# Source sums of a graph kernel with the message terms as weights, added up in transposed layout

## The reference

```python
h_edge = jnp.concatenate([x[src], x[dst]], axis=-1)
m_ij = jax.nn.relu(h_edge @ W_interact + b_interact)
m_i = jax.ops.segment_sum(m_ij, src, num_segments=x.shape[0])
m_i = m_i / jnp.asarray(math.sqrt(AVG_DEGREE), dtype=x.dtype)
out = x + jax.nn.relu((x + m_i) @ W_update + b_update)
```

## Time and profile before

| what | value |
|---|---|
| three timed runs | 1555.04, 1557.01, 1558.96 us; median 1557.01 |
| profiled execution, span from first to last instruction | 1552.8 us |
| PE, DVE, ACT, POOL busy | 85%, 87%, 61%, 60% of the span |

### The profile page before, as it was taken

How to read it: one execution, slowest core, us unless ns; L and a number is a source line. 1 busy time by engine, 2 the same in 40 slices (tenths; PEclk the granted TensorE clock), 3 DMA queues, 4 the chain that set the end, 5 groups by cost and what they waited for, 6 DMA issues and landing times.

```text
span 1552.8 us, 39671 instructions
## 1 busy us (share of the span) xinstructions
PE 1322.9 (85%) x14762; PEld 1128.6 (73%) x14762; DVE 1343.5 (87%) x3914; ACT 940.1 (61%) x1835; POOL 931.1 (60%) x942
## 2 busy tenths in 40 slices
PE   1512877999999989899999679889999999999997
PEld 1311655777777767677767578889899999998887
DVE  6968878999999945777866679999999999999998
ACT  2642766778777942010001358878888878887886
POOL 5253803777773005677770147777777777777773
PEclk9965889999999999999999789999999999999999
DMA  4003554475646218799987234444444444444442
GB/s 120 1 1 89 198 232 150 152 253 180 228 177 211 113 50 278 257 310 305 305 280 220 72 77 122 138 121 126 128 127 120 128 127 126 134 131 126 127 120 61
DMA packets 121785, 241.63 MB, mean 156 GB/s; under 512 B 20184, under 2 KB 74601, under 8 KB 121594
## 3 DMA queue, kind: packets, MB, share of 16 engines
q1 hardware_dynamic: 95179, 187.74, 36.1%
q0 software_dynamic: 24832, 50.78, 13.2%
q10 hardware_dynamic: 1584, 0.59, 0.1%
HBM read 169.09 MB, written 73.14 MB: 156 GB/s over the span
## 4 chain that ended last, share of the span: by engine, by line
PE 46%; DVE 35%; issue 7%; SPq 4%; DMA 4%; ACT 3%; POOL 2%; DVEq 1%; ACTq 0%; POOLq 0%
PE ps L1262 13%; PE ps L1468 12%; DVE room L2186 6%; PE ps L1244 5%; DVE hot L1809 4%; PE ps L1233 3%; PE ps L1479 3%; PE ps L1459 3%; DVE slab L2230 2%; SPq L663 2%; PE ps L1302 2%; DVE ps L2222 2%; DVE keys L1935 2%; DVE keys L1934 2%; DVE hot L1804 2%
## 5 line engine op out<-in xcount | busy, mean ns | idle before, releaser
L1014 ACT ACTIVATE slab<-ps 128x980 f16<-128x980 f32 x256 | 321.2, 1277 | 118.7 <-PE ps L1233 102.9
L925 POOL DMA_INDIRECT cells<-b_rows,work x236 | 245.1, 1039 | 74.9 <-issue 67.7
L1468 PE MATMUL ps<-slab,room 125*128 125x128 f16 x3538 | 236.0, 221 | 36.0 <-DVE room L2186 33.5
L1244 PE MATMUL ps<-slab,room 128*128 128x320 f16 x1568 | 252.2, 301 | 0.1
L1468 PEld LDWEIGHTS ps<-slab,room 125*128 125x128 f16 x3538 | 206.5, 98 | 49.5 <-DVE room L2186 49.1
L1123 ACT ACTIVATE lnw<-iota_w,keys 128x126 f32<-128x126 f32 x750 | 242.4, 389 | 0.0
L1459 PE MATMUL ps<-inv,hot 125*128 125x128 f16 x1800 | 224.3, 220 | 5.2 <-DVE hot L2176 5.1
L1262 PE MATMUL ps<-slab,room 128*128 128x320 f16 x1568 | 226.9, 301 | 0.0
L1233 PE MATMUL ps<-hot 128*128 128x245 bf16 x1024 | 160.6, 282 | 50.4 <-DVE hot L1809 39.0
L889 POOL DMA_INDIRECT hot<-t_rows,pairs x160 | 165.8, 1036 | 55.2 <-issue 48.1
L1262 PEld LDWEIGHTS ps<-slab,room 128*128 128x128 f16 x1568 | 153.2, 98 | 59.4 <-issue 2.7
(11 more groups left out here) (371 smaller groups left out, 2442.4 us busy)
## 6 DMA issues: line engine op xcount, KB each, us to landing
slabs_d<-slab SPq DMA_DIRECT2D x14, 3920.0 KB, 13.9
slab<-slabs_d SPq DMA_DIRECT2D x98, 560.0 KB, 5.5
hot<-lane_d SPq DMA_DIRECT2D x50, 576.0 KB
inv<-inv_row SPq DMA_DIRECT2D x32, 160.0 KB, 7.0
keys<-up_d SPq DMA_DIRECT2D x25, 160.0 KB
room<-up_d SPq DMA_DIRECT2D x25, 160.0 KB
cells<-b_rows,work POOLq DMA_INDIRECT x236
t_rows<-room SPq DMA_DIRECT2D x1, 3200.0 KB, 13.7
```

Of the source, the lines that this page charges most:

```text
L925: p.indirect_dma_start(rows_g[gi % RS][:, j, :], None, b_rows, bass.IndirectOffsetOnAxis(ap=node_t[:, t:t + 1], axis=0)).then_inc(e_gath[g ...
L1014: a.activation(slab[par][:, :, u * UB * BW:(u + 1) * UB * BW].rearrange("p h (k d) -> p k h d", k=UB), psum_unit(u).rearrange("p k (h d) - ...
L1244: last = t.matmul(ps[:, 4 + s % 2, 0:SC], table[:, h, term, :], slab[s % 2][:, h, :], start=k == 0, stop=k == HI * HALVES - 1)
L1468: last = t.matmul(to, end_hot[g // 3][0:BN, u:u + P], bt[0:BN, bt_at(tile, w), k, :], start=False, stop=w == w1 - 1 and k == HALVES - 1)
```

## The change

The source sum swaps its operands. Before, the source one-hot was the weights (128 edges by 126 nodes) and both message terms moved side by side (256 columns), which left the two terms in two halves, nodes on the partitions. Now each term is the weights (128 edges by 128 features) in a matmul of its own and the one-hot moves (125 columns); both terms add up in the same 125 columns of PSUM, features on the partitions. So `whole_sum` and `turn_sum` are gone, and `keep_sum` reads the bank directly, where `whole_sum` stood. The wait of `low_term` on `e_psum` is dropped too; the high term, for which it waits, has waited for the same count.

```diff
             def source_sum(gi):
                 b, g = divmod(gi, GB)
                 pe.wait_ge(e_low, gi + 1)
                 pe.wait_ge(e_dvehot if g in DVE_HOTS else e_srchot, hots(gi))
                 if g == 0 and b > 1:
-                    pe.wait_ge(e_whole, b - 1)
+                    pe.wait_ge(e_added, b - 1)
                 for j in range(GT):
-                    last = t.matmul(ps[0:BE, 4 + b % 2, 0:2 * D], src_hot[gi % 6][:, j, :],
-                                    msg[gi % 3][:, j, :, :].rearrange("p k f -> p (k f)"),
-                                    start=g == 0 and j == 0, stop=g == GB - 1 and j == GT - 1)
+                    for k in range(HALVES):
+                        last = t.matmul(ps[:, 4 + b % 2, 0:BN], msg[gi % 3][:, j, k, :], src_hot[gi % 6][:, j, 0:BN],
+                                        start=g == 0 and j == 0 and k == 0,
+                                        stop=g == GB - 1 and j == GT - 1 and k == HALVES - 1)
                 last.then_inc(e_psum, 1)
-
-            def turn_sum(b):
...
-                t.transpose(ps[:, 7, 2 * P:2 * P + BN], block_sum[0:BN, :], ident[0:BN, 0:BN]).then_inc(e_turned, 1)
...
-                if g == 2 and b > 1:
-                    turn_sum(b - 2)
...
             def low_term(gi):
                 dve.wait_ge(e_msg, gi + 1)
-                if gi > 2:
-                    dve.wait_ge(e_psum, gi - 2)
...
-            def whole_sum(b):
+            def keep_sum(b):
                 dve.wait_ge(e_psum, (b + 1) * GB)
-                if b:
-                    dve.wait_ge(e_turned, b)
-                v.tensor_reduce(out=block_sum[0:BN, :], in_=ps[0:BN, 4 + b % 2, 0:2 * D].rearrange("p (k f) -> p f k", k=2),
-                                op=ALU.add, axis=AX.X).then_inc(e_whole, 1)
-
-            def keep_sum(b):
-                dve.wait_ge(e_turned, b + 1)
                 to = hT[:, b * BN:(b + 1) * BN]
-                v.scalar_tensor_tensor(out=to, in0=ps[:, 7, 2 * P:2 * P + BN], scalar=settle[:, 0:1], in1=to,
+                v.scalar_tensor_tensor(out=to, in0=ps[:, 4 + b % 2, 0:BN], scalar=settle[:, 0:1], in1=to,
                                        op0=ALU.mult, op1=ALU.add).then_inc(e_added, 1)
...
-                if g == 2 and b > 1:
-                    keep_sum(b - 2)
                 if g == 4 and b:
-                    whole_sum(b - 1)
+                    keep_sum(b - 1)
...
             low_term(NGR - 1)
-            keep_sum(NB - 2)
-            whole_sum(NB - 1)
             keep_sum(NB - 1)
```

More of the change, by code:

```diff
@@ L395, in gnn_kernel @@
         g_hot = scaled[:, D:D + BN]
-        block_sum = scaled[:, 0:D]
         s_const = sem("s_const")
@@ L496, in gnn_kernel @@
         e_low = sem("e_low")
-        e_whole = sem("e_whole")
-        e_turned = sem("e_turned")
         e_psum = sem("e_psum")
@@ L1476, in source_sum @@
                 if g == 0 and b > 1:
-                    pe.wait_ge(e_whole, b - 1)
+                    pe.wait_ge(e_added, b - 1)
                 for j in range(GT):
-                    last = t.matmul(ps[0:BE, 4 + b % 2, 0:2 * D], src_hot[gi % 6][:, j, :],
-                                    msg[gi % 3][:, j, :, :].rearrange("p k f -> p (k f)"),
-                                    start=g == 0 and j == 0, stop=g == GB - 1 and j == GT - 1)
+                    for k in range(HALVES):
+                        last = t.matmul(ps[:, 4 + b % 2, 0:BN], msg[gi % 3][:, j, k, :], src_hot[gi % 6][:, j, 0:BN],
+                                        start=g == 0 and j == 0 and k == 0,
+                                        stop=g == GB - 1 and j == GT - 1 and k == HALVES - 1)
                 last.then_inc(e_psum, 1)
-            def turn_sum(b):
-                pe.wait_ge(e_whole, b + 1)
-                if b:
[L1487 to L1490, removed]
-                t.transpose(ps[:, 7, 2 * P:2 * P + BN], block_sum[0:BN, :], ident[0:BN, 0:BN]).then_inc(e_turned, 1)
             def update(c):
@@ L1509, in _ @@
                     general_edges()
-                if g == 2 and b > 1:
-                    turn_sum(b - 2)
                 if g == GB - 1 and b - 2 in LAST_BLOCK:
                     update(LAST_BLOCK.index(b - 2))
-            turn_sum(NB - 2)
             source_sum(NGR - 4)
@@ L1518, in _ @@
             source_sum(NGR - 1)
-            turn_sum(NB - 1)
             update(NC - 1)
```

## The result

Six timed runs of each kernel: 1555.38 us before (median, 1551.94 to 1558.96), 1544.77 after (1542.91 to 1549.98). The ratio, with its 95% interval, is 0.9935 [0.9918, 0.9952]: 0.65% or 10.1 us faster, between 7.5 and 12.8. The forecast was 6.2 us.

A forecast was written before the change was run, and what follows sets the result against it. The prediction took a loop of DVE and ACT to bound the third stage's ordinary blocks, with gathers close. 4.9 us (blocks to 48) + 1.3 (end) = 6.2 off the 1552.8 span, plus 4.2, gave 1550.8 us; range 1545.5 to 1555.

The forecast's parts named there:

- The loop: Third stage: DVE runs g2's low term to g5's row add, then ACT to g2's high term; blocks 8-48 gain 4.9 us.
- The wait in g2: Ordinary blocks, DVE's low term of g2 waiting for ACT's high term: 0.11 us becomes 0.37 in the block shown.
- the add in g2: DVE's add into `hT` leaves g2: its 0.26 us is worth nothing in ordinary blocks, counts fully in update blocks.
- The swap in g4: In DVE's half, the add (0.26 us) takes the reduction's place (0.33), shortening every block by 0.07 us.
- PE: Source sum on PE: six narrow matmuls at 56 ns take 0.50 us against 0.49 for three wide ones; no change.
- the slower rival: PE becomes the bound if narrow matmuls cost 98 ns each: 0.5 us more a block, 1577 us in all; 8%.
- The end: After the last row add: last high term starts 0.50 us earlier, final reduction and transposition drop out, 0.84; together 1.3 us.
- The step that failed: Blocks 0 to 7 of the third stage: nothing counted, as DVE's savings go into waiting for block 7's late gather.
- The base: Span of 1552.8 us and median of 1557.0, 4.2 above it; the same 4.2 was added to the changed kernel's span.
- The full gain: Rival: g2's low term does not wait for ACT, DVE gains 0.33 us in every block, POOL-capped at 10; 1545.7 us; 12%.
- The small part failing: Rival: the 0.07s are lost to g4's add cost or late gathers; 3.4 us left, 1553.6 us, no measurable change; 20%.

The follow-up runs named there:

- the two paddings: Changed kernel plus one add-sized DVE instruction on a scratch tile, at the end of g2 (1548.5 us, 0.9949) or in g4 ahead of the add (1558.7 us, 1.0013).
- the repeats: Unchanged kernels run again: before, second and third time, 1554.6 us (0.9983) and 1553.6 us (1.0); after, second time, 1545.7 us (0.995).
- The second timing: The changed kernel, unaltered, timed again against a copy of the kernel before on the same chip: 1545.7 us, 0.995, 7.8 us faster.
- the split early: ACT's split of `a` moved a block earlier, ahead of the high term of g5: on the changed kernel 1536.7 us (0.9892), on the kernel before 1551.1 us (0.9982).

## Why the prediction was right in its mechanism and short in its size

- **The loop** held. The wait in g2 was forecast as 0.37 us in the block shown and is 0.36 in one like it; the 0.26 of the add in g2 is worth nothing in ordinary blocks and all of it in update blocks, as the two paddings show. The swap in g4 is 0.08 a block where 0.07 was forecast. Forecast 4.9 us for blocks 8 to 48, measured 5.4, with 511.1 to 511.3 before and 505.7 to 505.9 after.
- **PE** held: six narrow matmuls step by 56 to 57 ns in the mean and cost what three wide ones did. Nothing in the traces speaks for the slower rival. The 81 ns of the Trainium skill (TensorE: Matmul & The Clock Gate, Back-to-back issue gap) are not what these matmuls took. PE has come near, though: in block 48 it holds up the row add of g3 by 0.32 us, in front of the longer wait for ACT.
- **The end** held: 1.4 us against 1.3, and the same up to the last add in the repeats.
- **The step that failed** is "For blocks 0 to 7 I count nothing: what DVE wins there it waits longer for the late gather in block 7." It took the gathers' arrival as given. In fact it moved: the waits for gathers are 4.5 to 5.7 us in three runs of before and 1.1 and 2.2 in two of after. Every kernel with the add, or a padding of its size, at the end of g2 and the row one-hot whole has 3.9 to 7.6 us of them, every one without has 0.6 to 2.2. In time that is 101.8 to 106.7 us for blocks 0 to 7 with the add there (mean of seven 103.7), 99.4 to 101.9 without (mean of five 100.4, the 2.8 of the update taken out). The first run of after lies high among these, at 101.9, since its row adds stood 3.4 us behind PE in block 3. Between before and after themselves it is some 3.0 us, on three executions and two: the term that the forecast put at nothing. With it the sum is 4.9 + 1.3 + 3.0 = 9.2, where 10.1 and 7.8 were measured. The gathers beside the row one-hots make up this difference: over 0.94 us each they took 3.9, 4.9 and 7.2 us in the runs of before, 2.0 and 1.9 in those of after. The padding in g2 bears this out less well: there they took 2.1, and what it lost in blocks 0 to 7 lies with other gathers.
- **The base** was off as well. The forecast stood on three runs with a median of 1557.0, 4.2 us above the span; six runs gave 1555.4, and a run lies 1.8 us above its own span. That put the predicted time 1.6 us too high, whatever the change did; with the gathers it took the measured 1544.8 to 0.7 us below the range. The second timing, 1545.7, lies just inside.
- **The full gain** gave 1545.7, nearly the measured time, by a mechanism that did not happen: it needs DVE not to wait for ACT, and DVE waits 11.9 us. The small part failing is out, too.

What stays open is how the add at the end of g2 makes the gathers later. That the row one-hot holds a gather that starts behind it is shown. That the add merely shifts when the two meet (it stands 0.26 us of DVE time ahead of the row one-hot) is not enough. Over the whole stage I took the gathers that start 0.27 to 0.31 us behind the start of a whole row one-hot. In the kernels without an add or padding at the end of g2 all 21 of them took 1.31 to 1.36 us. In those with one, 15 of 103 did, 77 took 1.53 to 1.55, and eleven, all in blocks 0 to 7, took 2.38 or 2.39. Block 7 with the split early shows it at the offset of 0.28 us at which the kernel before had 2.39:

```profile
1012.79 0.81 DVE L2163 TENSOR_SCALAR hot<-hot,lane_c 125x2304 f16<-125x2304 f16 x1
1013.07 1.34 POOL L922 DMA_INDIRECT cells<-b_rows,work  x1 [0.30 <-issue]
```

Nor does the period of a block separate the two sets: ordinary blocks take 11.80 to 12.25 us in the kernels with an add or padding there and 11.97 to 12.50 in those without, and the padding in g2 leaves them at the 12.17 of the changed kernel. What makes the difference at the same offset is not shown.

## What to carry to other kernels

When two engines set the pace in turn, ask of each saved instruction in which engine's half it stood: the same 0.26 us cost 2 us at one place and 11 at another, and moving one instruction of the second engine was worth 7.0 us, more than the 5.4 that the change gave in the same blocks. In a stage that waits for transfers saved work need not be lost: the arrival times can depend on the work that is moved. And before an instruction is moved to a later place, look for everyone who waits for its result.

## What the hardware did that I had not expected

An indirect gather issued by POOL takes 0.94 us alone. Those that started 0.15 to 0.45 us behind the start of one DVE instruction of 0.81 us on f16 data in SBUF ended 1.61 to 1.63 us behind that start, whatever their own start: 0.17 us behind it one took 1.45, 0.28 behind it 1.34, 0.39 behind it 1.23. All 79 of the kernels without an add or padding at the end of g2 did so, and 110 of the 203 of those with one; 80 ended 1.82 to 1.85 us behind it and 13 ended 2.66 to 2.68, with nothing in between. Cut into four pieces of 0.39 us the same work lets a gather through in 1.16 us or less.

The Trainium skill (SBUF — State Buffer, Who interferes with whom) says that a DVE instruction in one of its two-port modes, once it has the ports that it shares with GpSimd, blocks GpSimd for its whole length, and that descriptors made by GpSimd wait with it. The 1.61 to 1.63 agree with that, as 0.81 us of a gather's 0.94 are then left for after the instruction's end; the later ends go on beyond it, beside the short instructions that follow, and there the rule for one instruction is not enough. In which mode the row one-hot runs no trace here shows. The cut is dear: each added piece cost 0.17 us of DVE ((1.23 - 0.73) / 3).
